# A recommendation tower on one core: the order of units stands in a table, with layer matmuls beside transposes, turns nearer to their use and another share of sums on VectorE

## The chip, the cores and the metric
One core of one Trainium2 chip runs the whole program. The metric is the device time of one execution in microseconds, lower is better.

## What is computed
For each of B = 2048 samples, 32 embedding rows of 64 floats are gathered from 32 tables. For each of the 496 pairs (i, j) of features a bilinear form with its own 64x64 kernel gives one number; with 16 dense features these 512 numbers pass through a tower of three layers.

```python
e = jnp.stack([tbl_0[ids[:, 0]], ..., tbl_31[ids[:, 31]]], axis=1)      # 2048 x 32 x 64
kp = jnp.einsum('bpe,fpe,bpf->bp', p, kernel, q)    # p, q: rows i and j of each of 496 pairs
h = jnp.concatenate([kp, dense_ctx], axis=1)        # 2048 x 512
h = jnp.maximum(h @ W_top1 + b_top1, 0.0)           # 512
h = jnp.maximum(h @ W_top2 + b_top2, 0.0)           # 256
y = h @ W_top3
```

All data are float32.

## The kernel before, in words
The samples are cut into four **chunks** of 512 (four tiles of 128). Features go in 16 **pairs** of two; pair q holds features 2q and 2q + 1, 128 numbers a sample. In the rows below, PE is TensorE, PEld its loading of weights, DVE VectorE, ACT ScalarE, POOL GpSimd, SP SyncE.

- GpSimd (line 352) gathers the rows, pair after pair and chunk after chunk: eight indirect DMAs a pair (two features, four tiles), 128 rows each. Pairs 0 to 3 go to `kept_rows` (two chunks deep), pairs 4 to 15 to `rows`, a ring of four pairs: pair q waits until pair q - 4 has been turned (`unit_ready`), the first four of a chunk until the last four of the chunk before have.
- A **turn** (line 415) transposes a pair's rows on TensorE, four transposes of 128x128 a pair, one or two pairs a turn; VectorE copies the result to `xt` (line 684).
- A **duo** (lines 447 and 448) multiplies `xt` of pair q with the kernels of pairs (s, q): two matmuls of 64 input rows by 128 columns that run beside each other, moving 512 samples. VectorE multiplies the result with `xt` of pair s into `products` (line 667, ring of four). A special duo (lines 450 to 454, 64x64) serves the pairs of features inside blocks; 76 duos a chunk, 4 of them special.
- A **sum** (line 474) adds up the products of two duos over the 64 numbers, with a selector as weights (four matmuls of 128 rows by 32 columns, beside each other) into `sum_ps`; 38 a chunk. ScalarE copies a full bank to `z_sb` (line 567).
- A **batch** (lines 460 and 462) serves the pairs (s, q) with s < 4 and q > 3, for one tile: here `xt` is the weight and the kernels move. VectorE multiplies with `kept_rows` into `batch_products` (line 678, a ring of four batches); 48 batches a chunk. The product is summed either on ScalarE, in 16 activations with an accumulator (line 596), or on VectorE in one reduction (line 640). `DVE_SUMS` says which: every fourth batch of chunk 0 and every sixth of the others goes to VectorE, so 12, 8, 8 and 8.
- A **mix** (line 439) and a **batch turn** (line 428, called Z in the table of steps below) transpose those sums so that the tower can use them, once a chunk each.
- A **layer** step is one matmul of the tower of the chunk before (lines 490, 493, 496; 128 rows by 128 columns, the last two by 32). 26 of them a tower are strewn over the next chunk; ScalarE evacuates each of their 7 groups (lines 579, 581). The last chunk's tower stands alone at the end (lines 507 to 522).

Each matmul of float32 shows as two passes in the trace. Duos, batches, turns and batch turns are the **units**: unit g writes `y_ps[g % 3]` (three double banks of PSUM), so TensorE waits for VectorE to be through with unit g - 3 (`unit_done`).

`ORDER` is the list of all steps, made before the build; every engine walks through it and does its part, so it sets the order on all of them. Before, two functions make it by rules: `first_chunk` and `later_chunk`. A **burst** is four duos, then fill (turns, batches, layers), then two sums. In `later_chunk` up to two layer matmuls stand in a burst, one ahead of turns and batches, one behind them; turns come two pairs at a time at the bursts of `TURN_AT`; the first six pairs of the next chunk are turned in the last three bursts:

```python
        steps += layers[:1]
        del layers[:1]
        steps += fill
        while queue and queue[0] in turned:
            q = queue.pop(0)
            batches += [("batch", c, q, t) for t in range(CHUNK_TILES[c])]
        if layers and (b % 5 in SECOND or last and len(layers) > bursts - 1 - b):
            steps += layers[:1]
```

Of the kernel before, what the change touches and what calls it, by code (L numbers as in the profile page):

```python
# [15 lines left out]
CHUNK_TILES = (4, 4, 4, 4)  # L16
CHUNKS = len(CHUNK_TILES)
# [21 lines left out]
SPECIAL_BEHIND = {5: 0, 8: 1, 12: 2}  # L39


def tile_of(c, t):

    return sum(CHUNK_TILES[:c]) + t


def width(c):
    return CHUNK_TILES[c] * P
# [45 lines left out]
def first_chunk():  # L94


    steps, turned, done, quads, ahead, duos, batches = [], 0, 0, 0, 0, [], []
    queue = list(DUO)
    for q in range(PAIRS):
        if turned <= q:  # L100
            steps.append(("turn", 0, (q,)))
            turned = q + 1
        while queue and top_pair(queue[0]) <= q:
            duos.append(queue.pop(0))
        if q in BATCH_Q:
            batches += [("batch", 0, q, t) for t in range(CHUNK_TILES[0])]
        while duos or batches:
            if q >= WAITS and q < PAIRS - 1 and len(duos) < BURST and len(batches) < BURST:
                break
            burst = min(len(duos), BURST - done % 2)  # L110
            steps += [("duo", 0, a) for a in range(done, done + burst)]
            done += burst
            del duos[:burst]
            if q + 1 >= WAITS and q < PAIRS - 1 and len(duos) < BURST and turned == q + 1:
                steps.append(("turn", 0, (q + 1,)))
                turned = q + 2
            if q == PAIRS - 1 and len(duos) < 3 * BURST and ahead < AHEAD:
                steps.append(("turn", 1, (ahead, ahead + 1)))
                ahead += 2
            steps += batches[:FILL]  # L120
            del batches[:FILL]
            for quad in range(quads, done // 2):
                if quad == (Z_BANKS - 1) * Z_QUADS:
                    steps.append(("mix", 0))
                steps.append(("sum", 0, quad))
            quads = done // 2
    return steps


def later_chunk(c, layers):  # L130


    steps, turned, batches = [], set(range(AHEAD)), []
    queue = list(BATCH_Q)
    bursts, last = DUOS // BURST, c == CHUNKS - 1
    ends = bursts - 3 if last else bursts
    total = len(BATCH_Q) * CHUNK_TILES[c] + len(TURN_AT) + (1 if last else 1 + AHEAD // 2)
    placed = 0
    for b in range(bursts):
        steps += [("duo", c, a) for a in range(b * BURST, b * BURST + BURST)]  # L140
        fill = [("turn", c, (q, q + 1)) for q in TURN_AT if TURN_AT[q] == b]
        turned.update(q for turn in fill for q in turn[2])
        if b == 2:
            fill.append(("turn_batch", c - 1))
        if not last and b >= bursts - AHEAD // 2:
            first = AHEAD - 2 * (bursts - b)
            fill.append(("turn", c + 1, (first, first + 1)))
        if last and b == bursts - 1:
            fill.append(("turn_batch", c))
        placed += len(fill)  # L150
        while batches and placed < total * (b + 1) // ends:
            fill.append(batches.pop(0))
            placed += 1
        if b == LAYERS_FROM:
            layers += [("layer", c - 1) + piece for piece in LAYERS]
        steps += layers[:1]
        del layers[:1]
        steps += fill
        while queue and queue[0] in turned:
            q = queue.pop(0)  # L160
            batches += [("batch", c, q, t) for t in range(CHUNK_TILES[c])]
        if layers and (b % 5 in SECOND or last and len(layers) > bursts - 1 - b):
            steps += layers[:1]
            del layers[:1]
        for quad in range(2 * b, 2 * b + 2):
            if quad == (Z_BANKS - 1) * Z_QUADS:
                steps.append(("mix", c))
            steps.append(("sum", c, quad))
    assert not batches
    return steps  # L170


def work_order():

    order, layers = first_chunk(), []
    for c in range(1, CHUNKS):
        order += later_chunk(c, layers)
    assert not layers  # L180
    return order
# [45 lines left out]
def dlrm_tower(nc, ids, tables, pair_kernel, dense, w1, b1, w2, b2, w3, out):  # L227
    with ExitStack() as ctx:
# [67 lines left out]
        def landings(c):  # L296

            return 2 * 16 * sum(CHUNK_TILES[:c + 1])
# [435 lines left out]
```

## Time and profile before

| what | value |
|---|---|
| median of 3 runs | 830.16 us (830.12 to 830.24) |
| the profiled execution | 830.1 us |
| its span, first to last instruction | 827.9 us |
| mean granted clock of TensorE | 0.988 |
| TensorE busy | 765.6 us (92%) |
| VectorE busy | 653.6 us (79%) |
| ScalarE busy | 626.6 us (76%) |
| GpSimd busy | 484.0 us (58%) |

The span holds everything from the first to the last instruction of the profiled execution; 2.2 us lie around it. Busy time is the union of an engine's instructions. The parts that matter here are the timelines (start and length of single instructions, and in brackets how long the engine was idle before one and what ended that) and the tables by stretch.

### The profile page before, as it was taken

Reading aid. Unit: us, or ns where it says so; the run is one execution under the profiler, and the core shown is the slowest. Engines: PE = TensorE matmul, PEld = TensorE weight load, DVE = VectorE, ACT = ScalarE, POOL = GpSimd, SP = SyncE. Lnnn points to the kernel's source line nnn. Section 1 sums busy time; section 2 is a strip of 40 time slices with the busy share of each in tenths; the row PEclk is TensorE's granted clock in tenths of the full one; section 3 lists DMA queues with packets and bytes.
Section 4 is the critical chain, followed back from the end, with each engine's and each line's share of the span. In section 5 each row is a group of like instructions: output and inputs, shape, how many; then the busy total and the mean of one; then the engine's idle time right before and its main releaser. Section 6 shows DMA issues by size and latency. Waiting matters only on the chain.

```text
span 827.9 us, 14456 instructions
## 1 busy us (share of the span) xinstructions
PE 765.6 (92%) x3776; PEld 274.8 (33%) x3776; DVE 653.6 (79%) x580; ACT 626.6 (76%) x5033; POOL 484.0 (58%) x518
## 2 busy tenths in 40 slices
PE   0456799999989999999999999999999999999998
PEld 0122233333333333333433333333433333333333
DVE  0246799998869888889878888889878888888950
ACT  0019899876426789899886789899876899999942
POOL 6777777777777777777347777777147772000000
PEclk9988999999999999999999999999999999999999
DMA  9621212111322211121112211121012120010000
GB/s 332 201 51 28 53 27 53 27 29 28 54 53 51 53 28 29 33 48 28 15 40 54 44 35 28 32 49 27 8 39 53 27 54 10 2 27 2 1 1 0
DMA packets 33354, 36.26 MB, mean 44 GB/s; under 512 B 18420, under 2 KB 18676, under 8 KB 33144
## 3 DMA queue, kind: packets, MB, share of 16 engines
q0 software_dynamic: 16384, 16.81, 10.5%
q1 hardware_dynamic: 16888, 18.53, 7.7%
q8 instruction: 30, 0.49, 0.3%
q14 instruction: 52, 0.43, 0.2%
HBM read 26.91 MB, written 0.01 MB: 33 GB/s over the span
## 4 chain that ended last, share of the span: by engine, by line
PE 69%; POOL 12%; issue 10%; DVE 7%; ACT 1%; DMA 1%; DVEq 0%
PE y_ps L447 21%; PE y_ps L460 17%; PE sum_ps L474 13%; POOL rows L352 8%; PE layer_ps L490 6%; DVE products L667 5%; POOL kept_rows L352 4%; PE layer_ps L493 3%; PE y_ps L415 2%; PE y_ps L450 1%; DVE batch_products L678 1%; ACT batch_products L596 1%; PE y_ps L507 1%; DMA rows<-tbl_dram,idx 1%; DVE z_batch L640 1%
## 5 line engine op out<-in xcount | busy, mean ns | idle before, releaser
L596 ACT ACTIVATE batch_products<-batch_products 128x64 f32<-128x64 f32 x2496 | 596.4, 241 | 95.1 <-DVE batch_products L678 95.0
L596 ACT ACTIVATION_READ_ACCUMULATOR batch_products<-batch_products 128x1 f32 x2496 | 468.5, 188 | 0.0
L352 POOL DMA_INDIRECT rows<-tbl_dram,idx x384 | 362.4, 944 | 164.6 <-issue 112.7
L667 DVE TENSOR_TENSOR products<-y_ps,xt 128x1024 f32<-128x1024 f32 x288 | 333.4, 1216 | 81.9 <-PE y_ps L448 81.8
L447 PE MATMUL y_ps<-xt,kernel_sb 64*128 64x512 f32 x576 | 277.0, 617 | 11.4 <-DVE xt L684 9.3
L448 PE MATMUL y_ps<-xt,kernel_sb 64*128 64x512 f32 x576 | 277.1, 617 | 0.0
L678 DVE TENSOR_TENSOR batch_products<-y_ps,kept_rows 128x1024 f32<-128x1024 f32 x192 | 224.1, 1216 | 8.8 <-PE y_ps L462 4.1
L460 PE MATMUL y_ps<-kernel_sb,xt 64*128 64x512 f32 x384 | 190.9, 619 | 3.8 <-DVE products L667 2.8
L462 PE MATMUL y_ps<-kernel_sb,xt 64*128 64x512 f32 x384 | 190.9, 619 | 0.0
L447 PEld LDWEIGHTS y_ps<-xt,kernel_sb 64*128 64x128 f32 x576 | 102.0, 189 | 179.2 <-issue 112.3
L474 PE MATMUL sum_ps<-products,selector 128*32 128x512 f32 x1216 | 150.1, 604 | 1.8 <-DVE products L667 1.4
L352 POOL DMA_INDIRECT kept_rows<-tbl_dram,idx x128 | 120.9, 945 | 40.1 <-issue 37.5
L448 PEld LDWEIGHTS y_ps<-xt,kernel_sb 64*128 64x128 f32 x576 | 102.0, 189 | 0.0
L460 PEld LDWEIGHTS y_ps<-kernel_sb,xt 64*128 64x128 f32 x384 | 65.1, 188 | 108.3 <-DVE products L667 58.7
L684 DVE COPY xt<-y_ps 128x1024 f32<-128x1024 f32 (+1 forms) x40 | 40.1, 1003 | 43.7 <-PE y_ps L415 43.5
L474 PEld LDWEIGHTS sum_ps<-products,selector 128*32 128x32 f32 x1216 | 31.3, 109 | 103.3 <-issue 55.7
L462 PEld LDWEIGHTS y_ps<-kernel_sb,xt 64*128 64x128 f32 x384 | 65.1, 188 | 0.0
L596 ACT ACT_TABLE_LOAD x1 | 1.3, 1283 | 58.2 <-DVE batch_products L678 58.2
L640 DVE TENSOR_REDUCE z_batch<-batch_products 128x16 f32<-128x1024 f32 x36 | 43.6, 1210 | 0.2
L415 PE MATMUL y_ps<-identity,kept_rows 128*128 128x128 f32 x64 | 10.7, 313 | 32.4 <-DMA kept_rows<-tbl_dram,idx 32.4
L490 PE MATMUL layer_ps<-z_sb,w_sb 128*128 128x512 f32 x72 | 40.5, 645 | 0.0
L415 PE MATMUL y_ps<-identity,rows 128*128 128x128 f32 x192 | 27.8, 282 | 10.7 <-DMA rows<-tbl_dram,idx 10.7
(49 smaller groups left out, 279.4 us busy)
## 6 DMA issues: line engine op xcount, KB each, us to landing
special<-xt SPq DMA_DIRECT2D x64, 128.0 KB
kernel_sb<-pair_kernel_dram SPq DMA_DIRECT2D x15, 512.0 KB, 11.2
rows<-tbl_dram,idx POOLq DMA_INDIRECT x384, 2.4
kept_rows<-tbl_dram,idx POOLq DMA_INDIRECT x128, 2.4
w_sb<-w_dram SPq DMA_DIRECT2D x1, 1024.0 KB
w_sb<-w_dram SPq DMA_DIRECT2D x1, 512.0 KB
kernel_sb<-pair_kernel_dram SPq DMA_DIRECT2D x1, 256.0 KB, 3.0
z_batch<-dense_dram SPq DMA_DIRECT2D x16, 8.0 KB
```

What stands on the lines that cost most here:

```text
L352: pool.indirect_dma_start(rows_of(c, q, t)[:, h, :], None, tables[j], bass.IndirectOffsetOnAxis(ap=idx[:, n, j:j + 1], axis=0)).then_inc(k ...
L415: last = nc.tensor.transpose(y[:, n, t * P:(t + 1) * P], rows_of(c, q, t).rearrange("p h e -> p (h e)"), identity[:])
L447: nc.tensor.matmul(y[:, 0, :], kernel_sb[low, d, :], x_of(c, q)[low, :], start=True, stop=True)
L448: last = nc.tensor.matmul(y[:, 1, :], kernel_sb[high, d, :], x_of(c, q)[high, :], start=True, stop=True)
L460: nc.tensor.matmul(y[:, 0, :], x_of(c, q)[low, samples], kernel_sb[low, d:d + KEPT, :].rearrange("p d f -> p (d f)"), start=True, stop=True)
L462: nc.tensor.matmul(y[:, 1, :], x_of(c, q)[high, samples], kernel_sb[high, d:d + KEPT, :].rearrange("p d f -> p (d f)"), start=True, stop=T ...
L474: last = nc.tensor.matmul(sum_ps[32 * m:32 * m + 32, 0:width(c)], selector[:, 30 - 2 * s:62 - 2 * s], products[:, (duos + m // 2) % PRODUC ...
L490: last = nc.tensor.matmul(layer_ps[:, 0:width(c)], w1_sb[:, kb, n * P:n * P + P], z_of(c, kb), start=(kb == 0), stop=(kb == 3))
L596: last = nc.scalar.activation(product, product, ACT.Copy, accum_out=batch_sums(unit)[:, column:column + 1])
L640: nc.vector.tensor_reduce(batch_sums(unit), batch_products[:, BATCH_OF[unit] % BATCH_RING].rearrange("p b i e -> p (b i) e"), mybir.AxisLi ...
L667: nc.vector.tensor_tensor(products[:, duos % PRODUCT_RING, :, 0:width(c)], y[:, :, 0:width(c)], by, ALU.mult).then_inc(unit_done, 1)
L678: nc.vector.tensor_tensor(into, y[:], by, ALU.mult).then_inc(unit_done, 1)
```

## The change
`first_chunk`, `later_chunk` and their constants go. The same units, sums, mixes and layer matmuls are put in order by a table, `BURSTS`: each entry is a burst with five digits, the number of duos, of pairs turned, of layer matmuls ahead of the turns, of batches, and of layer matmuls behind the batches; a T adds the batch turn, which now stands behind the turns. Sums always follow at the burst's end. `burst_order` reads it:

```diff
-BURST = 4
-WAITS = 8
 GRAIN = 4
-FILL = 3
-LAYERS_FROM = 3
-SECOND = (0, 2)
-AHEAD = 6
-TURN_AT = {6: 0, 8: 2, 10: 4, 12: 7, 14: 10}
...
+DVE_SHARE = (3, 9, 6, 6)
+BURSTS = (
+    "04000 10000 20000 31000 01050 10020 11010 20040 01010 31040 41000 31030 41040 41030 40030 40020",
...
+)
...
     for q in range(1, PAIRS):
         own = [("block", s, q) for s in range(q) if s >= KEPT or q not in BATCH_Q]
+        if 1 < q < KEPT:
+            own[0:2] = own[1], own[0]
...
+    for burst in bursts:
+        duos, turns, before, fill, behind = map(int, burst[:5])
+        for unit in take(units, duos):
+            steps.append(unit)
+            if unit[0] == "quad" or unit[2] % 2:
+                quads.append((unit[1], unit_duos(unit)[-1] // 2))
+        steps += take(layers, before)
+        turned = take(pairs, turns)
+        batches += [("batch", g, q, t) for g, q in turned if q in BATCH_Q for t in tiles(g)]
+        while turned:
+            g, q = turned[0]
+            count = 2 if turned[1:2] == [(g, q + 1)] and (chunk(g) * PAIRS + q + 1) % XT_RING else 1
+            steps.append(("turn", g, tuple(q for _, q in take(turned, count))))
+        if burst[5:]:
+            steps.append(("turn_batch", towers))
+            towers += 1
+        steps += take(batches, fill)
+        steps += take(layers, behind)
...
-DVE_SUMS = {unit for n, unit in enumerate(BATCH) if n % (6 if unit[1] else 4) == 1}
+DVE_SUMS = {unit for n, unit in enumerate(BATCH) if n % DVE_SHARE[unit[1]] == 1}
```

`DVE_SHARE` gives every third batch of chunk 0 to VectorE, every ninth of chunk 1, every sixth of the others: 16, 5, 8 and 8. The first four pairs are turned in two turns of two before any duo; two duos of pairs 2 and 3 change places. Chunks may now be cut into segments, with a "quad" unit for half ones, but `SEGMENTS` holds four whole chunks, so no quad arises; semaphores of landed rows have a second set for them that is not used. All other steps and instructions are the same in kind and number (duos, batches, sums, transposes, layers); turns are 46 instead of 40, with single pairs more often.

On VectorE, at the start of chunk 0, from the copy of pair 4 on. Before (line 684 copies a turned pair, 678 multiplies a batch, 667 a duo, 640 sums a batch):

```order
L684 COPY xt<-y_ps 128x512
L678 TENSOR_TENSOR batch_products<-y_ps,kept_rows 128x1024 x4
L684 COPY xt<-y_ps 128x512
L667 TENSOR_TENSOR products<-y_ps,xt 128x1024
L667 TENSOR_TENSOR products<-y_ps,special 128x1024
L678 TENSOR_TENSOR batch_products<-y_ps,kept_rows 128x1024
L640 TENSOR_REDUCE z_batch<-batch_products 128x16
L678 TENSOR_TENSOR batch_products<-y_ps,kept_rows 128x1024 x2
L640 TENSOR_REDUCE z_batch<-batch_products 128x16
```

With the change (lines 722, 716, 705 and 670 are the same four):

```order
L722 COPY xt<-y_ps 128x512 x2
L716 TENSOR_TENSOR batch_products<-y_ps,kept_rows 128x1024 x5
L705 TENSOR_TENSOR products<-y_ps,xt 128x1024
L670 TENSOR_REDUCE z_batch<-batch_products 128x16
L716 TENSOR_TENSOR batch_products<-y_ps,kept_rows 128x1024 x2
L705 TENSOR_TENSOR products<-y_ps,special 128x1024
L722 COPY xt<-y_ps 128x512
L716 TENSOR_TENSOR batch_products<-y_ps,kept_rows 128x1024
L670 TENSOR_REDUCE z_batch<-batch_products 128x16 x2
```

The four batches of pair 4 stood between the turns of pairs 4 and 5; now both turns come first, and the batches of both pairs behind them.

On TensorE, in the second half of chunk 1, behind the four duos of a burst. Before:

```order
L490 MATMUL layer_ps<-z_sb,w1_sb 128x512
L460 MATMUL y_ps0<-kernel_sb,xt 128x512
L462 MATMUL y_ps0<-kernel_sb,xt 128x512
L460 MATMUL y_ps1<-kernel_sb,xt 128x512
L462 MATMUL y_ps1<-kernel_sb,xt 128x512
L460 MATMUL y_ps2<-kernel_sb,xt 128x512
L462 MATMUL y_ps2<-kernel_sb,xt 128x512
L490 MATMUL layer_ps<-z_sb,w1_sb 128x512
L474 MATMUL sum_ps<-products,selector 32x512 x8
```

With the change (516 is a layer, 431 the turn of one pair, 486 and 488 a batch, 500 two sums):

```order
L516 MATMUL layer_ps<-z_sb,w1_sb 128x512
L516 MATMUL layer_ps<-z_turned,w1_sb 128x512
L431 MATMUL y_ps1<-identity,rows 128x128 x4
L486 MATMUL y_ps2<-kernel_sb,xt 128x512
L488 MATMUL y_ps2<-kernel_sb,xt 128x512
L486 MATMUL y_ps0<-kernel_sb,xt 128x512
L488 MATMUL y_ps0<-kernel_sb,xt 128x512
L486 MATMUL y_ps1<-kernel_sb,xt 128x512
L488 MATMUL y_ps1<-kernel_sb,xt 128x512
L500 MATMUL sum_ps<-products,selector 32x512 x8
```

Two layer matmuls of a burst stood apart, with the batches between them; now they stand next to each other and to the turn.

## Rows read from the trace of the kernel before

**Rows 1.** The page, busy us (share of the span) and instructions.
```profile
PE 765.6 (92%) x3776; PEld 274.8 (33%) x3776; DVE 653.6 (79%) x580; ACT 626.6 (76%) x5033; POOL 484.0 (58%) x518
```

**Rows 2.** Stretches: length, PE, PEld, DVE, ACT, POOL busy, clock, DMA share, GB/s.
```profile
64.20:100.40 36.20, 27.04 (x116) 10.00 (x116) 26.40 (x25) 31.68 (x265) 27.37 (x29) 0.86 0.19 42
64.20:241.30 177.10, 164.58 (x848) 56.85 (x848) 157.28 (x143) 136.10 (x1117) 134.02 (x142) 0.97 0.19 40
100.00:147.00 47.00, 45.91 (x244) 14.97 (x236) 46.21 (x43) 45.25 (x379) 35.42 (x39) 1.00 0.18 38
244.00:803.00 559.00, 555.56 (x2792) 199.29 (x2792) 478.74 (x417) 479.16 (x3869) 301.04 (x319) 1.00 0.15 30
300.00:400.00 100.00, 100.00 (x493) 35.45 (x489) 87.73 (x77) 93.11 (x756) 75.48 (x80) 1.00 0.16 33
```

**Rows 3.** Timeline of POOL: start, length, instruction, idle before.
```profile
240.25 0.94 POOL L352 DMA_INDIRECT rows<-tbl_dram,idx  x1 [0.30 <-issue]
```

**Rows 4.** Timeline of PE: transposes that waited for rows.
```profile
64.20 1.08 PE L415 MATMUL y_ps<-identity,rows 128*128 128x128 f32 x4 [4.79 <-DMA rows<-tbl_dram,idx]
...
94.47 0.79 PE L415 MATMUL y_ps<-identity,rows 128*128 128x128 f32 x4 [2.38 <-DMA rows<-tbl_dram,idx]
...
243.92 0.66 PE L415 MATMUL y_ps<-identity,rows 128*128 128x128 f32 x4 [2.61 <-DMA rows<-tbl_dram,idx]
```

**Rows 5.** Timeline of PE, one burst of chunk 1.
```profile
298.67 0.69 PE L447 MATMUL y_ps<-xt,kernel_sb 64*128 64x512 f32 x1
...
301.35 0.59 PE L447 MATMUL y_ps<-xt,kernel_sb 64*128 64x512 f32 x1
...
301.77 0.59 PE L447 MATMUL y_ps<-xt,kernel_sb 64*128 64x512 f32 x1
...
302.30 1.13 PE L490 MATMUL layer_ps<-z_sb,w_sb 128*128 128x512 f32 x2
303.36 0.69 PE L460 MATMUL y_ps<-kernel_sb,xt 64*128 64x512 f32 x1
...
303.89 0.59 PE L460 MATMUL y_ps<-kernel_sb,xt 64*128 64x512 f32 x1
...
306.13 1.92 PE L474 MATMUL sum_ps<-products,selector 128*32 128x512 f32 x16
307.99 0.69 PE L447 MATMUL y_ps<-xt,kernel_sb 64*128 64x512 f32 x1
```

**Rows 6.** Timeline of PE, a layer matmul and a turn.
```profile
340.65 1.13 PE L490 MATMUL layer_ps<-z_sb,w_sb 128*128 128x512 f32 x2
341.61 1.04 PE L415 MATMUL y_ps<-identity,rows 128*128 128x128 f32 x8
342.58 0.69 PE L460 MATMUL y_ps<-kernel_sb,xt 64*128 64x512 f32 x1
```

**Rows 7.** The chain that ended last: start, length; the last tower's beginning.
```profile
803.11 10.50 PE y_ps L507 x24
```

**Rows 8.** Timeline of DVE in chunk 0, and the group of ScalarE's sums.
```profile
194.44 3.47 DVE L678 TENSOR_TENSOR batch_products<-y_ps,kept_rows 128x1024 f32<-128x1024 f32 x3
197.84 1.21 DVE L640 TENSOR_REDUCE z_batch<-batch_products 128x16 f32<-128x1024 f32 x1
198.96 1.21 DVE L667 TENSOR_TENSOR products<-y_ps,xt 128x1024 f32<-128x1024 f32 x1
...
L596 ACT ACTIVATE batch_products<-batch_products 128x64 f32<-128x64 f32 x2496 | 596.4, 241 | 95.1 <-DVE batch_products L678 95.0
```

**Rows 9.** Timeline of DVE and of PE where chunk 2's fifth batch comes.
```profile
446.11 1.22 DVE L678 TENSOR_TENSOR batch_products<-y_ps,kept_rows 128x1024 f32<-128x1024 f32 x1 [0.68 <-ACT batch_products L596]
...
449.65 0.69 PE L447 MATMUL y_ps<-xt,kernel_sb 64*128 64x512 f32 x1 [0.66 <-DVE products L667]
```

**Rows 10.** Timeline of ACT: its first instruction.
```profile
58.18 1.28 ACT L596 ACT_TABLE_LOAD   x1 [58.18 <-DVE batch_products L678]
```

More of the change, by code:

```diff
@@ L30, with chunk, tiles, half @@
 SPECIAL_BEHIND = {5: 0, 8: 1, 12: 2}
-BURST = 4
-WAITS = 8
 GRAIN = 4
-FILL = 3
-LAYERS_FROM = 3
-SECOND = (0, 2)
-AHEAD = 6
-TURN_AT = {6: 0, 8: 2, 10: 4, 12: 7, 14: 10}
[L39 to L48, printed above, removed]
+DVE_SHARE = (3, 9, 6, 6)
+BURSTS = (
[6 rows of a table added]
+)
+def chunk(g):
+    return SEGMENTS[g][0]
+def tiles(g):
+    return range(SEGMENTS[g][1], SEGMENTS[g][2])
+def half(g):
+    return len(tiles(g)) < TILES
+def columns(g):
+    return slice(SEGMENTS[g][1] * P, SEGMENTS[g][2] * P)
+def first_of(c):
+    return min(g for g in range(len(SEGMENTS)) if chunk(g) == c)
+def last_of(c):
+    return max(g for g in range(len(SEGMENTS)) if chunk(g) == c)
 def stored_duos():
@@ L91, in top_pair @@
     return duo[2] if duo[0] == "block" else 4 * duo[1] + 3
[L94 to L126, printed above, removed]
-    return steps
@@ L130, in later_chunk @@
[L130 to L170, printed above, removed]
@@ L173, in work_order, with units_of, unit_duos @@
[L173 to L181, printed above, removed]
-ORDER = work_order()
-UNIT = [step for step in ORDER if step[0] in ("duo", "batch", "turn", "turn_batch")]
+def units_of(g, quad):
+    pair = (2 * quad, 2 * quad + 1)
+    if half(g) and all(DUO[a][0] == "block" for a in pair):
+        return [("quad", g, quad)]
+    return [("duo", g, a) for a in pair]
+def unit_duos(unit):
+    return (unit[2],) if unit[0] == "duo" else (2 * unit[2], 2 * unit[2] + 1)
@@ new lines, in burst_order, with take @@
+def burst_order(bursts):
+    units = [unit for g in range(len(SEGMENTS)) for quad in range(QUADS) for unit in units_of(g, quad)]
+    pairs = [(g, q) for g in range(len(SEGMENTS)) for q in range(PAIRS)]
+    steps, layers, batches, quads, towers = [], [], [], [], 0
+    def take(queue, count):
+        assert count <= len(queue)
+        taken = queue[:count]
+        del queue[:count]
+        return taken
+    for burst in bursts:
[16 more added lines that the diff above has]
+        steps += take(layers, behind)
+        for g, quad in take(quads, len(quads)):
+            if quad == (Z_BANKS - 1) * Z_QUADS:
+                steps.append(("mix", g))
+            steps.append(("sum", g, quad))
+            if quad == QUADS - 1 and g == last_of(chunk(g)) and chunk(g) < CHUNKS - 1:
+                layers += [("layer", chunk(g)) + piece for piece in LAYERS]
+    assert not (units or pairs or batches or layers or quads) and towers == CHUNKS
+    return steps
@@ L186 @@
+ORDER = burst_order(" ".join(BURSTS).split())
+UNIT = [step for step in ORDER if step[0] in ("duo", "quad", "batch", "turn", "turn_batch")]
 UNIT_OF = {step: g for g, step in enumerate(UNIT)}
 TURN_OF = {(unit[1], q): g for g, unit in enumerate(UNIT) if unit[0] == "turn" for q in unit[2]}
+DUO_UNIT = {(unit[1], a): unit for unit in UNIT if unit[0] in ("duo", "quad") for a in unit_duos(unit)}
+PRODUCT = [unit for unit in UNIT if unit[0] in ("duo", "quad")]
+PRODUCT_OF = {unit: n for n, unit in enumerate(PRODUCT)}
@@ L472, in add_up @@
                 last_bank = kb == Z_BANKS - 1
                 for m in range(4):
-                    last = nc.tensor.matmul(sum_ps[32 * m:32 * m + 32, 0:width(c)], selector[:, 30 - 2 * s:62 - 2 * s],
-                                            products[:, (duos + m // 2) % PRODUCT_RING, m % 2, 0:width(c)],
+                    slot, place = product_of(g, 2 * quad + m // 2)
+                    last = nc.tensor.matmul(sum_ps[32 * m:32 * m + 32, columns(g)], selector[:, 30 - 2 * s:62 - 2 * s],
+                                            products[:, slot, m % 2, place],
@@ L618, in _ @@
                 del open_sums[:len(ready)]
-                if kind in ("duo", "batch", "turn", "turn_batch"):
+                if kind in ("duo", "quad", "batch", "turn", "turn_batch"):
                     g += 1
@@ L637, in sum_batch @@
                 dve.wait_ge(unit_done, UNIT_OF[unit] + 1)
[L638 removed]
+                if chunk(unit[1]) and unit[2] < BATCH_Q[MIXED]:
                     dve.wait_ge(mixed, unit[1])
```

288 lines of the change are left out of this document (162 added, 126 removed), and 5 rows, old and new, of the table BURSTS.

## The prediction

> **What bounds the kernel now.** I read the busy times first, then stretches, then single starts. Over the span TensorE is busy 92%, VectorE 79%, ScalarE 76% [rows 1]. That average hides two regimes [rows 2]. From 244 to 803 us TensorE is busy 555.6 of 559 us and VectorE 86%: TensorE's own list sets the pace. From 100 to 147 us VectorE is busy 46.2 of 47 us: there it is the equal or the bound. Both regimes hang on the gathers. One starts every 0.94 + 0.30 = 1.25 us [rows 3], a pair of features needs eight, so a pair lands every 10.0 us. TensorE's transposes waited for rows at 64.20, at 94.47 and, for pair 7 of chunk 1, at 243.92 (2.61 us) [rows 4]. From 94.47 (pair 8) to that pair are 15 pairs, 150 us: 244.4, which is where it stands. GpSimd never paused before it, so **no order starts the turn of chunk 1's pairs 6 and 7 before about 244**. I cut the time there. Up to it the change can only lose; what is behind it is the gain.
>
> **Behind 244: TensorE's list.** The same steps follow the cut in both orders: 212 block duos, 12 special ones, 144 batches, 114 sums, 78 layer matmuls, transposes of 42 pairs, mixes and batch transposes. A pass of 512 columns takes 0.43 us (301.35 to 301.77), a duo, batch, layer or sum two. What differs is how often the array changes its tile shape. In [rows 5] one burst (4 duos, a layer, 3 batches, 2 sums) runs from 298.67 to 307.99: 9.32 us for 10 steps of 0.853, so 0.79 us for 4 changes, **0.197 us each**. The starts show where it sits: last duo pass to layer 0.53 instead of 0.43, layer to batch 1.06 instead of 0.85, first batch pass 0.53. A turn directly behind a layer costs no second one: 340.65 to 341.61 is 0.96 and 341.61 to 342.58 is 0.97 for 0.85 each, two ends for both together [rows 6]. Counted in the two lists from the cut on, the changes of shape (64x128, 64x64, 128x128, 128x32) fall from 261 to 237. In all, the 78 layer matmuls form 78 stretches before and 58 after; 19 of them touched a turn, 28 do now. 24 x 0.197 = **4.7 us** less.
> The Trainium skill (TensorEngine Tiling, Tiling Modes) says that changing the tiling mode, "not just tile", drains TensorE; these rows agree, 0.197 us a change and none between turn and layer. By a drain alone for every change the gain would be the same 24.
>
> **Behind 244: waits.** All steps at 0.427 a pass are 498.8 us, 261 changes 51.4; the tower starts at 803.11 [rows 7], 559.2 after the cut. So 9.0 us are waits. The first three bursts behind the cut hold about 4.2 of them: they have no layer matmul, so VectorE (1.13 us a product or sum, 3 in 3.40 from 194.44 to 197.84, [rows 8]) falls behind TensorE's 0.85, and one puts five batches in one burst. In chunks 2 and 3 that burst costs 0.15 and the next 0.9: at 446.11 the fifth product waits 0.68 us for ScalarE (2496 sums in 596.4 us [rows 8], so 16 take 3.82 a batch; the ring holds four), and at 449.65 TensorE 0.66 for VectorE [rows 9]. The three mixes cost 1.3, the last bursts 1.3. The table never puts five batches behind each other there and starts chunk 1's batches one burst earlier. I keep the mixes at 1.3 and take 0.9 for the first bursts, 0.8 where four batches follow a batch transpose, 0.8 at the end and 1.0 elsewhere: **4.8**, so 4.2 less. Bounds: 1.3 (the mixes only) and 9.0 (all stay). I take the middle, since the burst with five goes but bursts with 10.8 us of VectorE work on 10.7 of TensorE's are new.
> Where turns now stand singly and late, a gather may be late. The tightest place: chunk 2's pairs 8 and 9 need the slots of 4 and 5. Between those turns the list has 12 duos, 2 batches, 5 layers and 6 sums (25 x 0.853), two single turns (0.85) and 11 changes (2.2): 24.4 us. Two pairs and a landing need 20.0 + 2.4 (the last gather before 243.92 starts eight starts of 1.25 behind the pair's first, so about 241.5). Hidden, by 2 us.
>
> **Up to 244.** Before, TensorE came to the cut at 241.3 and waited. Now pair 4's four batches stand behind pair 5's turn (64.2). Before, they ran in front of it, and ScalarE began at 58.18 [rows 10]. The table leaves ScalarE and VectorE empty for 10 us, and gives VectorE four more sums (16, not 12): behind 64.2 VectorE has 4 + 4 operations of 1.13 more, 157.3 [rows 2] + 9.1 = 166.4 us. Walked with these durations:
> (a) The first product is ready at 68.3: the turn's 1.1 us, two passes of 0.85, a product of 1.2 (behind idle stretches TensorE is granted half its clock for a while: 0.86 on average from 64.2 to 100.4 [rows 2]). The batch ring ties VectorE to ScalarE: the 17th batch needs the 13th summed, ScalarE's ninth, 68.3 + 9 x 3.82 = 102.7; with it and two sums VectorE is at 106.2.
> (b) 31 duos, 21 batches, 7 sums and 5 copies keep VectorE busy 69.8 us, with some 2 us idle for pairs 10 and 11 (landing 114.5, 124.4): 178.2.
> (c) Four more duos, then VectorE has caught up and TensorE leads, from the end of its sums at 185.0: 55 duos, batches and sums (46.9), 8 pairs turned and a mix (3.8), 22 changes (4.3), together 55.0 us to the cut, plus 4.4 for waits (before, 0.4 to 1.1 in each of seven such bursts): **244.4**.
> So the slack of 2.6 us is used up and the cut stands 0.5 later. Bounds: 243.9 (the rows) and 254.9. The latter takes VectorE's share before, from 64.2 to 100.4 (26.4 of 36.2 us, 73% [rows 2]), for the 36.3 us of work it now has up to the same duo, 49.8 us, then the 140.9 us that followed. I take the walk, since VectorE reached 98% [rows 2] where it had a stock of work.
>
> **Sum.** 244.4 + 498.8 + 237 x 0.197 (46.7) + 4.8 + 24.8 (tower, 803.11 to 827.9, unchanged) = 819.5 of span, against 827.9: -8.4. The profiled execution took 830.1 with that span, and the median is 830.16; with the same 2.2 around it 821.7, say **822.0**. 0.2% (1.7 us) is about what a measurement of this kernel can tell from no change.
>
> **Rivals.**
> 1. The waits stay (9.0): every burst still alternates VectorE's backlog and idling. For: bursts with 10.8 us of VectorE work. Against: from 300 to 400 us, with a layer matmul in every burst, TensorE was busy all 100 us [rows 2]. 821.7 + 4.2 = 825.9.
> 2. The late start is not recovered: the cut at 254.9 by the bound above. For: the ring held VectorE before. Against: ScalarE has 32 batches in chunk 0 instead of 36. 821.7 + 10.5 = 832.2, at the border of no change and slower.
> 3. **Slower: ScalarE in chunk 1.** VectorE sums only 5 of its 48 batches (8 before). 43 x 3.82 = 164.3, with 12 evacuations of some 0.65 us 172 us, in about the 170 that TensorE's list leaves from the first batch's product to the last's. It decides if ScalarE can't be full: at the 93% of its busiest stretch, 300 to 400 us [rows 2], 172 becomes 185, +12.8: 834.5. For: the ring of four couples it to VectorE. Against: counted batch by batch, the latest of its sums comes 1.1 us after TensorE reaches the batch that needs its buffer.
> 4. The change gives no fewer drains, because a change of shape is hidden where weights are fetched ahead: then only the waits go, 821.7 + 4.7 = 826.4. Against: the gaps of [rows 5] stand at every change there.
>
> **Chances.** Forecast 0.65 (818 to 825), rival 1 0.15, rival 2 0.08, rival 3 0.06, rival 4 0.06. Forecast and rivals 1 and 4 lie below 828.5: faster 0.86. Rival 2 is split, 0.05 within 0.2% and 0.03 slower. Rival 3 may be milder than its price: 0.04 of it slower, 0.02 no change. So 0.07 for no change and 0.07 for slower. The range starts at 818.0 (waits of 1.3 only) and reaches to 829.0, beyond rivals 1 and 4 and short of 2 and 3.
>
> **What would show it.** The turn of chunk 1's pairs 6 and 7 at 243.9 to 245, with a wait for rows below 2 us; a longer wait means that the walk priced chunk 0 too high, a start after 252 is rival 2. Bursts of 4 duos, layer, 3 batches and 2 sums still at 9.32. The last tower at 794 to 796. ScalarE busy 93 to 98% from 250 to 410, VectorE seldom waiting for it; TensorE waiting for products there for more than 5 us in total is rival 3. In chunk 2 no wait of transposes for rows above 1 us. I'm wrong if the cut-to-tower stretch is not 549 to 552.

## The result, and the profile after

The changed kernel takes **820.39 us** (median of 4 runs, 820.20 to 820.45), the kernel before beside it 830.14 (4 runs, 829.94 to 830.24): a ratio of 0.9882, with an interval of 0.9865 to 0.990. The forecast was 822.0 in a range of 818.0 to 829.0, with 0.86 on faster. The profiled execution took 820.40 with a span of 818.6.

Busy times on the page of the changed kernel, which answer to [rows 1]:

```profile
PE 754.0 (92%) x3776; PEld 275.7 (34%) x3776; DVE 654.2 (80%) x587; ACT 620.9 (76%) x5001; POOL 484.0 (59%) x518
```

Its stretches, which answer to [rows 2] (length, then the busy time of PE, PEld, DVE, ACT and POOL, then clock, DMA share, GB/s):

```profile
64.20:100.40 36.20, 28.35 (x124) 10.50 (x125) 30.22 (x29) 31.52 (x255) 27.36 (x29) 0.93 0.19 42
64.20:241.30 177.10, 164.22 (x844) 55.99 (x844) 162.49 (x147) 125.79 (x1027) 133.97 (x142) 0.98 0.18 37
100.00:147.00 47.00, 43.17 (x220) 14.50 (x218) 43.71 (x41) 36.23 (x304) 35.42 (x39) 0.96 0.18 38
244.00:794.00 550.00, 549.28 (x2805) 203.05 (x2802) 478.99 (x426) 489.30 (x3966) 301.05 (x319) 1.00 0.15 32
300.00:400.00 100.00, 100.00 (x498) 36.90 (x494) 86.61 (x77) 96.03 (x785) 75.49 (x80) 1.00 0.18 38
```

Behind the cut TensorE is busy all but 0.7 of 550 us, where 3.4 of 559 were idle. From 100 to 147 us VectorE has fallen from 46.2 to 43.7. The timeline of TensorE, its turns of rows at the first pair behind pair 4 and at the cut (they answer to [rows 4]), and the chain that ended last ([rows 7]):

```profile
64.42 1.09 PE L431 MATMUL y_ps<-identity,rows 128*128 128x128 f32 x4 [7.30 <-DMA rows<-tbl_dram,idx]
...
245.28 1.09 PE L431 MATMUL y_ps<-identity,rows 128*128 128x128 f32 x8
...
793.80 10.50 PE y_ps L533 x24
```

The cut is at 245.28, 1.36 later than before, and now without a wait for rows. From there to the last tower are 548.5 us, 10.7 fewer than the 559.2 of before. 1.36 - 10.7 = -9.3 is the whole difference of the spans (827.9 to 818.6).

Two cautions for the comparisons below. Before, pair 6's transposes had run at 240.65, ahead of the wait, and the cut at 243.92 is the start of pair 7's; with the change both pairs stand behind 245.28. Over the same steps, from the one behind the turn (244.51 before, 246.36 now) to the tower, the gain is 11.2 us, against 1.9 lost ahead of it. And the chain puts the tower's start 0.07 us behind TensorE's timeline, which has 803.03 before and 793.73 now; experiments are compared by the timeline.

One burst of the changed kernel behind the cut, on TensorE, which answers to [rows 5]:

```profile
325.33 0.69 PE L464 MATMUL y_ps<-xt,kernel_sb 64*128 64x512 f32 x1
...
328.44 0.59 PE L464 MATMUL y_ps<-xt,kernel_sb 64*128 64x512 f32 x1
...
328.96 1.13 PE L516 MATMUL layer_ps<-z_sb,w_sb 128*128 128x512 f32 x2
...
330.02 0.69 PE L486 MATMUL y_ps<-kernel_sb,xt 64*128 64x512 f32 x1
...
332.80 1.92 PE L500 MATMUL sum_ps<-products,selector 128*32 128x512 f32 x16
334.65 0.69 PE L464 MATMUL y_ps<-xt,kernel_sb 64*128 64x512 f32 x1
```

325.33 to 334.65 is 9.32 us, what the same burst took before. So no step got cheaper: what got fewer are changes of shape and waits.

**What stood at the cut before.** Two stretches of the kernel before, just behind its wait of 2.61 us [rows 4]:

```profile
244.00:246.00 2.00, 2.00 (x16) 0.89 (x20) 1.22 (x1) 0.00 (x0) 1.70 (x2) 0.74 0.18 40
246.00:248.00 2.00, 2.00 (x13) 0.34 (x4) 0.00 (x0) 0.00 (x0) 1.39 (x3) 0.50 0.08 17
```

and TensorE's timeline there:

```profile
244.51 3.23 PE L474 MATMUL sum_ps<-products,selector 128*32 128x512 f32 x16
247.67 1.04 PE L447 MATMUL y_ps<-xt,kernel_sb 64*128 64x512 f32 x1
248.54 0.59 PE L447 MATMUL y_ps<-xt,kernel_sb 64*128 64x512 f32 x1
```

The third number from the end of a stretch is the granted clock: 0.74, then 0.50. Right behind the wait TensorE was put from 2.4 to 1.2 GHz; ahead of the wait it had been busy at 1.00, and four transposes stand on either side of it. Sixteen sum passes took 3.16 us from start to start (1.85 in the burst above) and the first duo pass 0.87 instead of 0.53: **1.6 us lost to the clock**, beside the 2.61 waited. The same stretches of the changed kernel, with the clock at 1.00 throughout:

```profile
244.00:246.00 2.00, 2.00 (x15) 1.10 (x12) 2.00 (x3) 0.00 (x0) 1.62 (x2) 1.00 0.74 185
246.00:248.00 2.00, 2.00 (x10) 0.74 (x10) 2.00 (x3) 0.00 (x0) 1.39 (x3) 1.00 0.09 17
```

### The profile page after: what moved, and what is told of

Read it like the earlier page. It is cut to its first block, busy times and chain, and to the rows that moved or that the text cites. A ratio compares the mean times of both kernels' runs of the same rounds, so it can differ in the third digit from the quotient of the medians.

```text
span 818.6 us, 14440 instructions
## 1 busy us (share of the span) xinstructions
PE 754.0 (92%) x3776; PEld 275.7 (34%) x3776; DVE 654.2 (80%) x587; ACT 620.9 (76%) x5001; POOL 484.0 (59%) x518
## 4 chain that ended last, share of the span: by engine, by line
PE 77%; DVE 8%; issue 6%; POOL 5%; ACT 3%; DMA 1%; DVEq 0%; ACTq 0%
PE y_ps L464 26%; PE y_ps L486 18%; PE sum_ps L500 15%; PE layer_ps L516 6%; POOL kept_rows L371 4%; DVE products L705 4%; PE layer_ps L519 3%; DVE batch_products L716 3%; PE y_ps L431 3%; ACT batch_products L626 2%; POOL rows L371 2%; PE y_ps L467 2%; PE y_ps L533 1%; PE y_ps L542 1%; DVE z_batch L670 1%
## 5 line engine op out<-in xcount | busy, mean ns | idle before, releaser
L464 PE MATMUL y_ps<-xt,kernel_sb 64*128 64x512 f32 x576 | 272.1, 609 | 2.9 <-DVE products L705 2.3
L465 PE MATMUL y_ps<-xt,kernel_sb 64*128 64x512 f32 x576 | 272.1, 609 | 0.0
L464 PEld LDWEIGHTS y_ps<-xt,kernel_sb 64*128 64x128 f32 x576 | 100.7, 187 | 170.9 <-issue 93.9
L465 PEld LDWEIGHTS y_ps<-xt,kernel_sb 64*128 64x128 f32 x576 | 100.7, 187 | 0.0
L722 DVE COPY xt<-y_ps 128x512 f32<-128x512 f32 (+1 forms) x46 | 40.8, 891 | 54.6 <-PE y_ps L431 54.5
L516 PE MATMUL layer_ps<-z_sb,w_sb 128*128 128x512 f32 x72 | 38.1, 631 | 0.0
```

Of the source, the lines that this page charges most:

```text
L464: nc.tensor.matmul(y[:, 0, :], kernel_sb[low, d, :], x_of(g, q)[low, :], start=True, stop=True)
L465: last = nc.tensor.matmul(y[:, 1, :], kernel_sb[high, d, :], x_of(g, q)[high, :], start=True, stop=True)
L516: last = nc.tensor.matmul(layer_ps[:], w1_sb[:, kb, n * P:n * P + P], z_of(c, kb), start=(kb == 0), stop=(kb == 3))
```

## The experiments

All of them start from the changed kernel. The first four ran on one chip (the kernel before 830.58 there), the next four on another (830.73), so each is best read by its ratio to the kernel before beside it; the changed kernel's is 0.9882. Except for the shares of sums, which some name, they only reorder the same steps. Of each table only the beginning of what changed is shown; "..." stands for the rest.

**1. Chunk 0 of before, the rest of the change.**

```
-DVE_SHARE = (3, 9, 6, 6)
+DVE_SHARE = (4, 9, 6, 6)
-    "04000 10000 20000 31000 01050 10020 11010 20040 01010 31040 ...
+    "01000 01000 11000 20000 01000 30000 01040 01000 20030 00010 ...
```

> Up to the turn of chunk 1's pairs 6 and 7 (the cut) the order and VectorE's share of sums of before, behind it those of the change. Theory (two independent parts, joined at a cut that the gathers bound): the cut at 243.9 us with a wait for rows of 2 to 3 us again, the stretch from there to the last tower 548.5 us as with the change, so 1.4 us faster than the change: 819.0. Rival (the late start of chunk 0 pays for itself, since VectorE and ScalarE enter chunk 1 with less behind them): 820.4 or more, and the stretch behind the cut longer than 549.5.

Measured: 820.06 us (818.48 to 821.5, 4 runs), ratio 0.9874 (0.9857 to 0.989). Timeline of TensorE, the two turns at the cut and the first tower matmul:

```profile
240.34 0.66 PE L431 MATMUL y_ps<-identity,rows 128*128 128x128 f32 x4
243.91 0.66 PE L431 MATMUL y_ps<-identity,rows 128*128 128x128 f32 x4 [2.92 <-DMA rows<-tbl_dram,idx]
...
793.02 1.98 PE L533 MATMUL y_ps<-z_sb,w_sb 128*128 128x512 f32 x4
```

The old chunk 0 stands at its rows 2.92 us. It loses the clock too, as before (0.50 from 246 to 248 us), 1.2 us in the burst behind the wait. From the next burst on (250.83, in the changed kernel 251.54) both take the same 542.2 us to the tower: the two parts are independent. Its tower starts 0.7 us before the changed kernel's; the two medians cannot be told apart.

**2. The change's chunk 0, the rest of before** is the other half (with before's share of chunk 1 too).

```
-DVE_SHARE = (3, 9, 6, 6)
+DVE_SHARE = (3, 6, 6, 6)
     "... 41040 41030 40030 40020 41040 40020 40010 42000 40030 42010 40020 40030 41000 43000",
-    "42030 40020 41030 41230T 51000 30240 41130 ...
+    "42000 40050 42010T 40130 ...
```

> Up to the cut the change's order and share, behind it those of before. Theory: the cut at 245.3 without a wait for rows, 559.2 us to the last tower, so 831.1 us: slower than before by about 1. Rival (part of the stretch of 559.2 was a consequence of the wait at the cut): the stretch below 557, 829 or less.

Measured: 830.55 us (830.11 to 830.61, 10 runs), ratio 0.9998 (0.9989 to 1.0008). Timeline of TensorE, cut and tower:

```profile
245.29 1.09 PE L431 MATMUL y_ps<-identity,rows 128*128 128x128 f32 x8
...
803.11 1.98 PE L533 MATMUL y_ps<-z_sb,w_sb 128*128 128x512 f32 x4
```

**All of the gain is behind the cut**, as the prediction had it. The new chunk 0 brings nothing. But it costs nothing either, though the cut stands later. From the step behind the turn to the tower the old order takes 556.8 us here (246.31 to 803.11) and took 558.5 before (244.51 to 803.03). Of these 1.7 us, 1.3 lie in the first burst: the clock that is not lost here, which was on neither side of the prediction. The other 0.4 is a second wait for rows of the kernel before, which TensorE comes too late to meet here:

```profile
283.93 0.66 PE L415 MATMUL y_ps<-identity,rows 128*128 128x128 f32 x4 [0.21 <-DMA rows<-tbl_dram,idx]
```

Without both, the waits behind the cut are 557.8 - 498.8 - 51.4 = 7.6 us, not 9.0.

**3. Twelve joined layers parted again** (the same work, 10 changes of shape more).

```
-    "... 40020 41030 41230T 51000 30240",
-    "41130 42220 41110 40130 40330 ...
+    "... 40020 41030 41131T 51000 30141",
+    "41130 42121 41110 40130 40231 ...
```

> The change with 12 of its joined layer matmuls parted again: the second of two ahead of the batches goes behind them. The array changes its tile shape 247 instead of 237 times behind the cut. Theory (0.197 us for each change of shape): 2.0 us slower than the change, 822.4. Rival (joining brought nothing, the gain is only fewer waits of VectorE and ScalarE): 820.4, within 0.3.

Measured: 821.53 us (821.41 to 822.63, 4 runs), ratio 0.9895 (0.9879 to 0.9912), so 1.1 us over the change by the ratios. In this execution chunk 0 was 1.3 us shorter. From the end of the first burst behind the cut to the tower (250.25 to 794.78, against 251.54 to 793.73) it is 544.5 instead of 542.2: 2.3 us for 10 changes, where 2.0 were expected. Compared burst by burst, ten are longer, each by one change: nine of them by 0.20 us, which is the price of the list, and the tenth (from 267.50, the one with a batch turn) by 0.60, since TensorE also waits 0.34 there for VectorE ahead of its first batch (273.50), which one layer covers less well than two. All other bursts behind the first take what they took.

**4. The leading layers between a burst's second and third duo** instead of between duos and batches.

```
-        for unit in take(units, duos):
+        for place, unit in enumerate(take(units, duos)):
+            if place == 2:
+                steps += take(layers, before)
+                before = 0
```

> The change with every burst's leading layer matmuls moved between its second and third duo, away from the turns. There are 59 stretches of layer matmuls instead of 58, but 292 changes of tile shape instead of 237. Theory (the price is per change of shape, and a turn beside a layer saves one): 55 x 0.197 = 10.8 us slower than the change, 831.2. Rival (the price is per stretch of layer matmuls, for their weights of 128 rows, wherever they stand): 820.6, within 1.

Measured: 838.84 us (838.03 to 839.89, 4 runs), ratio 1.0098 (1.0081 to 1.0115). That is 18 us over the change, neither the 10.8 of the theory nor the 0.2 of the rival. The burst that was shown above, on TensorE:

```profile
327.68 0.69 PE L467 MATMUL y_ps<-xt,kernel_sb 64*128 64x512 f32 x1
...
329.60 1.13 PE L519 MATMUL layer_ps<-z_sb,w_sb 128*128 128x512 f32 x2
330.65 0.69 PE L467 MATMUL y_ps<-xt,kernel_sb 64*128 64x512 f32 x1
...
333.76 0.59 PE L489 MATMUL y_ps<-kernel_sb,xt 64*128 64x512 f32 x1
334.24 0.69 PE L489 MATMUL y_ps<-kernel_sb,xt 64*128 64x512 f32 x1
...
335.30 1.92 PE L503 MATMUL sum_ps<-products,selector 128*32 128x512 f32 x16
337.15 0.69 PE L467 MATMUL y_ps<-xt,kernel_sb 64*128 64x512 f32 x1
```

It has four changes as before (a duo and a batch have the same shape) and still takes 9.47 instead of 9.32: at 334.24 a pass comes 0.48 behind the one before instead of 0.43, and the next 0.53. Five units now follow each other behind the layer, and VectorE, at 1.13 us each, falls behind TensorE's 0.85. All bursts behind the cut were compared one by one. In 22 the layers now stand apart from batches only; they are longer by 4.5 us together, 0.21 each, and 20 of them have no change of shape more. In 25 a turn of rows or of batches stood behind the layers; they are longer by 12.9, 0.52 each, and 23 of them have two changes more. (0.52 - 0.21) / 2 = 0.16 us a change, near the 0.197 of the list. Bursts without a layer take what they took. So 0.21 at each of 47 bursts, about half of the loss, is not changes of shape, but **the place of the layer**. How much it is goes by the batches that follow: in the 20 bursts without a new change it is 0.00 us with two batches, 0.15 with three and 0.43 with four. Behind the duos the layer covers VectorE's backlog, in front of them it doesn't.

**5. The old shares of sums in the new order.**

```
-DVE_SHARE = (3, 9, 6, 6)
+DVE_SHARE = (4, 6, 6, 6)
```

> The changed kernel's order with the old shares (4, 6, 6, 6): VectorE sums 12 batches of chunk 0 (16 in the change) and 8 of chunk 1 (5), ScalarE the rest. Theory (orders and mode changes do it, chunk 0 is VectorE's): 4 sums fewer, 4 x 1.21 = 4.8 us less for VectorE ahead of the cut, so TensorE is at the turn of chunk 1's pairs 6 and 7 earlier than 245.3 and waits there for its rows until about 243.9; behind it 3 sums more, 3.6 us, on a VectorE that was idle 20 of 165 us. Stretch from the cut to the tower still 548.5, total 819 (817.5 to 821). Rival (the share of chunk 1 was the gain, since ScalarE or VectorE limits there): the stretch grows to 552 or more, total 823 and over.

Measured: 821.75 us (821.72 to 821.85, 4 runs), ratio 0.9891 (0.9876 to 0.9906). Cut 245.93, tower 794.76: 548.8 us between them, against 548.5. So five or eight of chunk 1's sums on VectorE are the same to 0.4 us. Chunk 0 did not get faster by 4.8 us, it got 0.65 slower. Timeline of VectorE there:

```profile
86.31 2.35 DVE L716 TENSOR_TENSOR batch_products<-y_ps,kept_rows 128x1024 f32<-128x1024 f32 x2
89.41 1.22 DVE L716 TENSOR_TENSOR batch_products<-y_ps,kept_rows 128x1024 f32<-128x1024 f32 x1 [0.76 <-ACT batch_products L626]
93.23 1.23 DVE L716 TENSOR_TENSOR batch_products<-y_ps,kept_rows 128x1024 f32<-128x1024 f32 x1 [2.59 <-ACT batch_products L626]
```

VectorE waits 3.4 us for buffers that ScalarE still sums; in the changed kernel it sums one more itself and waits for none in this stretch. TensorE waits with it and loses the clock (0.50 from 96 to 100 us, 1.00 in the changed kernel). The share of three belongs to the late start of ScalarE (68.87 instead of 58.18 [rows 10]). It was needed for the new table rather than a gain by itself.

**6. Pair 4's batches ahead of pair 5's turn again.**

```
-    "04000 10000 20000 31000 01050 10020 ...
+    "04000 10000 20000 31040 01010 10020 ...
```

> Pair 4's four batches stand ahead of pair 5's turn, as in the kernel before. ScalarE's first sum at 58 to 60 us instead of 70. Theory: TensorE's arrival at the cut was set by the late first sums and the ring; it comes earlier, but can't start before its rows have landed, 243.9. Stretch behind it 548.5 as before. Total 819.0, a wait for rows of up to 2.5 us at the cut. Rival (VectorE's list sets chunk 0 whenever ScalarE starts): the cut stays at 245.3 and the total at 820.4 or above.

Measured: 820.06 us (818.61 to 820.33, 4 runs), ratio 0.9866 (0.9851 to 0.9881). Timeline of TensorE at the cut:

```profile
241.80 0.66 PE L431 MATMUL y_ps<-identity,rows 128*128 128x128 f32 x4
244.15 0.66 PE L431 MATMUL y_ps<-identity,rows 128*128 128x128 f32 x4 [1.69 <-DMA rows<-tbl_dram,idx]
```

TensorE comes 3.5 us earlier (241.80 for 245.28), waits 1.69 and then runs at half clock again. The burst ends at 251.06, the changed kernel's at 251.54: of 3.5 us 0.5 are left, and from there both take the same 542.2 us to the tower. It is the theory, with 1.2 us of clock on top, and in the medians nothing of it can be seen.

**7. As 6, and the turn of chunk 1's pairs 6 and 7 one burst later.**

```
-    "... 43000 42030 40020 41030 41230T ...
+    "... 43000 40030 42020 41030 41230T ...
```

> As the kernel with pair 4's batches early, and the turn of chunk 1's pairs 6 and 7 stands one burst later, behind the burst with pair 4's batches: what waits for rows there is moved behind 9 us of other work, so no wait for rows at 244 us is left. 233 changes of mode instead of 237 behind the cut (-0.8). If TensorE was held at the cut by rows, the total is 1 to 3 us under that of the kernel with the early batches: 817 (815.5 to 819). If it wasn't held, the two agree within 1 us.

Measured: 819.64 us (817.17 to 819.97, 4 runs), ratio 0.9858 (0.9843 to 0.9873). There is no wait for rows at the cut any more, and the clock stays at 1.00, but the median is 0.4 under that of 6 instead of 1 to 3. In the profiled execution the burst ahead of the cut ended at 240.67 instead of 238.16, though the order up to there is the same. Here TensorE came earlier to pair 10's rows, waited 3.32 us for them at 114.26 and then had clock 0.50 from 116 to 120 us; in 6 it waited 1.37 at 114.30 and the clock stayed at 1.00. Chunk 0 falls out differently from execution to execution (a run of 817.17 stands beside three near 819.8), and this hides in the totals what the turn brings. The traces do show it: from that burst's end to the tower are 552.1 us (240.67 to 792.76), against 555.1 in 6 (238.16 to 793.26). That is 3.0 us: the wait of 1.7, the clock's 1.2 and one change of shape.

**8. The old chunk 0 of 1, with the turn of chunk 1's pairs 6 and 7 one burst later.** The edits of 1 and 7 together.

> Chunk 0 in the order and with the share of the kernel before, everything behind as in the change, and the turn of chunk 1's pairs 6 and 7 one burst later. With that turn in its old place TensorE stood 2.92 us for rows at 243.9 and the total was 820.06. Theory (rows alone hold it): no wait for rows there, 820.06 - 2.9 = 817.1 (816 to 818), the tower at 790. Rival (the time saved is lost at the next turn of rows, or to VectorE's backlog): tower at 793, total 820.

Measured: **816.35 us** (815.39 to 816.81, 5 runs), ratio 0.9827 (0.9813 to 0.984). This is faster than both kernels, and 3.7 us under 1. Timeline of TensorE, turn and tower:

```profile
249.09 1.09 PE L431 MATMUL y_ps<-identity,rows 128*128 128x128 f32 x8
...
788.62 1.98 PE L533 MATMUL y_ps<-z_sb,w_sb 128*128 128x512 f32 x4
```

and its stretches where 1 stood still:

```profile
241.00:245.00 4.00, 4.00 (x26) 1.02 (x24) 4.00 (x5) 1.51 (x13) 3.09 (x4) 1.00 0.13 25
245.00:249.00 4.00, 4.00 (x24) 1.28 (x20) 3.25 (x4) 4.00 (x36) 3.08 (x4) 1.00 0.20 38
```

in 1 they were

```profile
241.00:245.00 4.00, 1.08 (x6) 0.82 (x8) 1.90 (x3) 0.00 (x0) 2.99 (x4) 0.96 0.12 25
245.00:249.00 4.00, 4.00 (x16) 1.31 (x13) 2.83 (x3) 1.22 (x11) 2.88 (x4) 0.62 0.15 29
```

The tower starts 4.4 us earlier. The two bursts at the cut take 17.5 us (236.53 to 254.05) instead of 21.7 (236.71 to 258.46): 2.9 of the wait, 1.1 of the clock and 0.2 for one change of shape. The other 0.2 was there ahead of them, and what follows takes 534.6 us in both. (The four changes that the expectation of 7 counts come of counting from a turn one burst further on; over the same steps it is one.) That no order starts this turn before about 244 held; what the prediction made of it, that chunk 0 can only lose, did not. The turn can be moved behind other work.

**9 to 12. The change once more, twelve layers moved to the next burst (twice), and all turns one burst earlier.** These ran on two further chips, the second time of the moved layers on one and the rest on the other, and on both the kernel before took 1276 us. Of the two edits, the moved layers:

```
-    "41130 42220 41110 40130 40330 40120 ...
+    "41130 42220 41010 40230 40330 40020 ...
```

and the earlier turns:

```
-    "... 42030 40020 41030 41230T 51000 30240 ...
+    "... 42030 41020 41030 41230T 50000 31240 ...
```

> The changed kernel itself, unaltered, beside the others on this chip, where the kernel before took 830.6 to 830.7 (830.14 where the change was first timed). Expected: 0.9882 of it, 820.9 (820 to 821.5).

> Twelve times behind the cut, two bursts that follow each other with one layer matmul each become one without and one with two. The same work and 10 changes of mode less (227 instead of 237). Theory (what the change brought is above all that a burst's layer stands between its duos and its batches, 1 us in which VectorE catches up with the ring of buffers; a burst of 4 duos, 3 batches and 2 sums takes 8.78 without a layer and 9.32 with one, 10.18 with two): taking it out gives back 0.54, the second costs 0.86, 12 x 0.32 = 3.8 us slower than the change, and up to 8 where a turn stands in the burst too: 824.7 (823.5 to 829). Rival (changes of mode alone count): 2 us faster than the change, 818.9.

> The order with twelve layers moved one burst back, a second time, since all engines stood still for tens of us together on the chip of the first time (the kernel before took 1276 us there). Theory (a layer between duos and batches gives VectorE time to catch up): 12 x (0.86 - 0.54) = 3.8 us slower than the change, up to 8 with the turns: ratio to the kernel before 0.9928 (0.9915 to 0.998), 824.3 where that takes 830.2, with waits of TensorE for VectorE in the bursts without a layer. Rival (changes of mode alone): 2 us faster than the change, ratio 0.986.

> Every turn behind the cut one burst, 7 to 12 us, earlier; all else as in the change (239 changes of mode instead of 237). Theory (turns close to their use are no part of the gain): rows come from GpSimd at a fixed pace of 8 x 1.25 = 10 us a pair, and pairs 8, 9 and 10 of chunk 1, turned at 262.8, 274.3 and 284.7 in the change, have landed about 10 us before, so waits for rows stay under 1.5 us in all and the total is within 1 us of the change, 819.9 to 821.9. Rival (turns come too early for their rows): waits for rows of 1 us or more at each of some ten turns, total 826 and over.

Measured: the change 1269.36 us, ratio 0.9961 (0.9943 to 0.998); layers moved 1278.79, ratio 1.002 (1.0 to 1.004), and 1277.48, ratio 1.0031 (1.0006 to 1.0055); turns earlier 1259.85, ratio 0.9884 (0.9845 to 0.9923). None of these totals is near what was expected, that of the unaltered change least of all. On these chips TensorE, VectorE and ScalarE stand nearly still for 10 to 50 us at a time. Timeline of ScalarE in such a stretch of the change:

```profile
411.33 0.26 ACT L626 ACTIVATE batch_products<-batch_products 128x64 f32<-128x64 f32 x1 [1.20 <-issue]
412.04 0.20 ACT L626 ACTIVATION_READ_ACCUMULATOR batch_products<-batch_products 128x1 f32 x1 [0.46 <-issue]
413.43 0.26 ACT L626 ACTIVATE batch_products<-batch_products 128x64 f32<-128x64 f32 x1 [1.19 <-issue]
```

Its instructions come up to 1.4 us apart, with nothing that the profile shows to wait for; on the other chips such a pair takes 0.24 to 0.26 us. Busy time grew far less than the span (PE 852.0 for 754.0, more of it at half clock; DVE 661.3, ACT 656.2). GpSimd alone goes on: in the long standstills it gathers at its full pace (from 210 to 240 us 7.56 of every 10 us busy, TensorE 0.7 on average), and where it pauses (340 to 370) TensorE is busy 99%. That is a coincidence in time, with exceptions; no run separates the two, and why is open.

The totals are a weak answer to the question that the runs were for. The moved layers are 9.4 us slower than the change on the same chip, with intervals that don't touch, but a standstill is longer than that. Bursts without a standstill say more, and they repeat: the changed kernel's are as long as on the first chip (10.18 and 9.76, for instance), and those of the two runs with moved layers agree with each other to 0.02 us. TensorE's starts of a burst that lost its layer, and of the next, with two:

```profile
600.63 0.64 PE L467 MATMUL y_ps<-xt,kernel_sb 64*64 64x512 f32 x1
...
608.25 0.69 PE L464 MATMUL y_ps<-xt,kernel_sb 64*128 64x512 f32 x1
...
611.88 1.98 PE L516 MATMUL layer_ps<-z_sb,w_sb 128*128 128x512 f32 x4
613.79 0.69 PE L486 MATMUL y_ps<-kernel_sb,xt 64*128 64x512 f32 x1
...
619.28 0.69 PE L464 MATMUL y_ps<-xt,kernel_sb 64*128 64x512 f32 x1
```

7.62 for 8.62 in the change, and 11.03 for 10.18. Ten of the twelve bursts that lost a layer ran undisturbed and were shorter by 5.4 us together, 0.54 each. A layer that stands alone in its burst costs 0.54 us, less than its own two passes (0.85), since TensorE would otherwise have waited for VectorE. Eight that gained one ran undisturbed: four are longer by 0.86 each, the other four by 1.0, 1.2, 2.0 and 2.3. In the last two, the two layers that now stand together belong to different groups, and the second waits for ScalarE to evacuate the first, behind its queue of sums (second run, the burst at 901.07):

```profile
904.70 1.12 PE L516 MATMUL layer_ps<-z_turned,w_sb 128*128 128x512 f32 x2
907.00 1.12 PE L516 MATMUL layer_ps<-z_sb,w_sb 128*128 128x512 f32 x2 [1.18 <-ACT h_sb L609]
```

With 0.86 for every gain, twelve moves cost 12 x (0.86 - 0.54) = 3.8 us, the theory's number; with the mean of all eight (1.24) they cost 8.4, the "up to 8" of its range, though for another reason than turns. Either way they lose, though there are ten changes of shape fewer. No undisturbed run shows the total. In the kernel with earlier turns no turn behind the cut waited for rows, but the standstills gave the rows more time. It is 9.5 us faster than the change there, and whether that is the turns or the standstills stays open, as does whether "turns close to their use" matters.

## Why the prediction was right

- **The cut.** "The cut stands 0.5 later", at 244.4, with no wait: 245.28, no wait. The walk's points: ScalarE's first instruction 68.87 (first product forecast 68.3); the end of (b) 179.1 for 178.2; TensorE's sums of (c) 186.4 for 185.0; from there 58.9 for 59.4. The 0.9 us too little arose up to the end of (b).
- **Changes of shape.** "24 x 0.197 = 4.7 us" stands: the burst still takes 9.32, and parting layers cost 0.20 us a change in nine bursts of ten. The Trainium skill (TensorEngine Tiling (Array Packing), Tiling Modes) has TensorE drained at each change of mode. Experiments 3 (0.20 to 0.23 a change) and 4 (0.16) agree that each change costs time; the drain itself is not seen.
- **Waits.** This term was mis-sized on both sides: "4.8, so 4.2 less". Measured are 548.5 - 498.8 - 46.7 = 3.0. Three things were wrong in the 9.0 of before. First, 1.3 to 1.6 was TensorE's clock behind the wait for rows. The prediction put it to VectorE: "they have no layer matmul, so VectorE (...) falls behind". Second, the 498.8 hold 42 pairs of transposes, but pair 6's had run ahead of 243.92, so before it should have been 9.4. Third, "the three mixes cost 1.3" is no wait: a mix is eight passes of 128 columns, and the 498.8 come out only with four. In the changed kernel:

```profile
402.08 1.16 PE L456 MATMUL sum_ps<-identity,z_batch 128*128 128x128 f32 x8
403.17 1.92 PE L500 MATMUL sum_ps<-products,selector 128*32 128x512 f32 x16
```

From 402.08 to 403.17 are 1.09 us: 0.85 for the passes and 0.2 for a change. This stands on both sides and so did no harm to the forecast. The 3.0 are then 1.7 us of waits. Compared burst by burst with the list, 1.3 stand in the first three bursts behind the cut (forecast 0.9) and 0.6 in the last (0.8); no other burst is off by more than 0.11 either way (1.8 were forecast there). The order of before has 6.3 in experiment 2: 2.9 in the first three bursts, 1.8 around the two with five batches, 1.5 in the last ones. 6.3 - 1.7 = 4.6 of waits and 4.7 of changes are the 9.3 us between the two stretches (557.8 and 548.5). The bursts "with 10.8 us of VectorE work on 10.7 of TensorE's" cost nothing; each has a layer in front of its batches, and experiment 4 shows what it costs to take that away. Which of the table's moves took away which wait was not tested one by one.

- **The sum.** Forecast 821.7, measured 820.4: +0.9 at the cut, -1.8 of waits, -0.4 around the span (1.8 instead of 2.2, which nothing here explains). The first two partly cancel. The stretch from cut to tower, 548.5, lies half a microsecond under the 549 to 552 outside of which I had called myself wrong: the mechanism held, the waits were sized too high.
- **The rivals.** 1: the waits did not stay. 2: no late cut. 3: ScalarE was busy 96% from 300 to 400 us, and from 250 to 410 us TensorE was idle 0.4 us in all; by experiment 5 the share of chunk 1 is worth 0.4 us at most. 4: the changes of shape count.
- **Right for a reason that was too narrow.** "Up to it the change can only lose" took the place of the turn as given. Experiment 8 is 4 us faster than the change, by moving it.

## What to carry to other kernels

Where a transfer sets the earliest start of one step, don't only speed up what stands ahead of it: put work that doesn't need it in between, since the wait costs its length and, behind it, TensorE's clock (here 2.6 us and 1.6). Small matmuls that nobody waits for are best spread over the bursts, between what loads the slower engine and what loads it next, even where gathering them in every other burst would save changes of shape (here 0.54 us for one alone, 0.86 and more for a second). Within a burst, where two stand there anyway, they are cheaper side by side (0.20 us), and a turn between such matmuls of the same shape comes free of changes. Before adding up what an order saves, count the same steps on both sides: a cut that moves by half a turn, or a step listed with half its passes, is worth as much as a wait.

## What the runs showed that I had not expected

- A wait of 1.7 us (experiment 6), 2.6 (before) or 2.9 (experiment 1) for rows, out of 100% busy at 2.4 GHz, was followed by a stretch at 1.2 GHz (clock 0.50 from 246 to 248 us in each). A wait of 0.49 us at the same place (experiment 3, 245.03) and one of 1.37 at 114.30 (experiment 6) were not.
- The same order of steps ended chunk 0 up to 2.5 us apart in two kernels (experiments 6 and 7), and single runs of them differ by 2.8 us, while behind the cut the same bursts repeat to a few hundredths of a microsecond.
- Two chips took 1276 us for a kernel of 830, with engines that stood without a wait that the profile shows, and single bursts between the standstills as fast as elsewhere. The ratio of 0.9882 became 0.9961 there.
